# An attention and FP4 feed-forward layer, tile by tile: turning the quantised codes with a transposing DMA instead of TensorE, and moving three small pieces of work between engines

## The reference

```
q = elu(x Wq + bq) + 1;  k = elu(x Wk + bk) + 1, each head scaled to length 1;  v = x Wv + bv
attn = (q k^T) v per head of 16;  y = x + attn Wo + bo
x1 = layernorm(x + (layernorm(y, 1e-6) * gamma + beta))
fq(a): per block of 16 along the last axis: scale = max|a| / 6; each a/scale rounded to 0, .5, 1, 1.5, 2, 3, 4, 6 with its sign; times scale
h = silu(fq(x1) fq(w_gate)^T) * (fq(x1) fq(w_up)^T)        # 704 wide
out = layernorm(x1 + fq(h) fq(w_down)^T)
```

## Time and profile before

| | |
|---|---|
| median of 3 runs | 700.19 us (700.13 to 703.07) |
| the profiled execution | 700.59 us, of which 698.9 us from the first to the last instruction |
| busy PE, DVE, ACT, Pool | 683.4, 584.1, 489.3, 608.8 us |
| DMA traffic | 56.36 MB |
| granted TensorE clock | 0.998 of full |

### The profile page before, as it was taken

How to read it: one execution, slowest core, us unless ns; L and a number is a source line. 1 busy time by engine, 2 the same in 40 slices (tenths; PEclk the granted TensorE clock), 3 DMA queues, 4 the chain that set the end, 5 groups by cost and what they waited for, 6 DMA issues and landing times.

```text
span 698.9 us, 14240 instructions
## 1 busy us (share of the span) xinstructions
PE 683.4 (98%) x4370; PEld 602.8 (86%) x4370; DVE 584.1 (84%) x1441; ACT 489.3 (70%) x954; POOL 608.8 (87%) x947
## 2 busy tenths in 40 slices
PE   8999999999989999999999999999999999999995
PEld 6888888888868799999999999999999999999995
DVE  6678678876778899889989998998998998998774
ACT  4677777766777676777677677677767767767664
POOL 3988898988888998899989989899899988989766
PEclk9999999999999999999999999999999999999999
DMA  8544443344301111122211122122111211100001
GB/s 267 189 136 136 136 140 117 131 157 155 107 32 34 58 47 46 45 78 75 76 66 57 36 86 80 57 76 76 46 61 62 77 45 47 61 17 16 21 28 45
DMA packets 23135, 56.36 MB, mean 81 GB/s; under 512 B 2642, under 2 KB 5908, under 8 KB 23060
## 3 DMA queue, kind: packets, MB, share of 16 engines
q1 hardware_dynamic: 22640, 55.32, 23.4%
q10 hardware_dynamic: 420, 0.13, 0.1%
HBM read 30.22 MB, written 25.17 MB: 79 GB/s over the span
## 4 chain that ended last, share of the span: by engine, by line
PE 91%; DVE 2%; POOL 2%; issue 2%; ACT 1%; DMA 1%; SPq 0%; POOLq 0%; DVEq 0%
PE banks L407 23%; PE banks L408 22%; PE banks L409 22%; PE banks L553 8%; PE banks L524 7%; PE banks L445 2%; PE banks L418 2%; PE banks L567 1%; PE banks L566 1%; PE banks L431 1%; PE banks L476 1%; DMA arena<-in_L_attn_x_dram 1%; PE banks L484 1%; POOL arena L1164 1%; DVE actT_lo L958 0%
## 5 line engine op out<-in xcount | busy, mean ns | idle before, releaser
L407 PE MATMUL banks<-wgu_hi,actT_lo 128*128 128x512 f32 (+1 forms) x384 | 149.8, 390 | 1.6 <-DVE actT_lo L958 1.4
L408 PE MATMUL banks<-wgu_lo,actT_hi 128*128 128x512 f32 (+1 forms) x384 | 144.0, 375 | 0.0
L409 PE MATMUL banks<-wgu_hi,actT_hi 128*128 128x512 f32 (+1 forms) x384 | 143.3, 373 | 0.0
L725 ACT ACTIVATE arena<-banks 128x512 f32<-128x512 f32 x64 | 38.4, 600 | 111.8 <-PE banks L409 111.6
L1164 POOL TENSOR_TENSOR arena<-arena 128x960 f32<-128x960 f16 (+2 forms) x68 | 115.3, 1695 | 0.0
L1140 POOL TENSOR_TENSOR arena<-arena 128x704 f32<-128x704 f32 x64 | 91.8, 1434 | 20.5 <-DVE arena L945 18.6
L407 PE MATMUL banks<-wd_hi,actT_lo 128*128 128x256 f32 x320 | 100.1, 313 | 0.0
L958 DVE TENSOR_TENSOR actT_lo<-banks,actT_hi 128x512 fp32r<-128x512 f32 (+1 forms) x132 | 85.5, 674 | 16.9 <-ACT actT_hi L711 16.2
L409 PE MATMUL banks<-wd_hi,actT_hi 128*128 128x256 f32 x320 | 90.2, 282 | 0.0
L408 PE MATMUL banks<-wd_lo,actT_hi 128*128 128x256 f32 x320 | 90.2, 282 | 0.0
L407 PEld LDWEIGHTS banks<-wgu_hi,actT_lo 128*128 128x128 f32 x384 | 72.5, 189 | 11.2 <-DVE actT_lo L958 2.3
(11 more groups left out here) (126 smaller groups left out, 1917.3 us busy)
## 6 DMA issues: line engine op xcount, KB each, us to landing
xs<-x_plus_scratch SPq DMA_DIRECT2D x32, 512.0 KB, 3.3
x_plus_scratch<-xs SPq DMA_DIRECT2D x24, 512.0 KB, 2.9
arena<-in_L_attn_x_dram SPq DMA_DIRECT2D x32, 256.0 KB, 3.5
out_dram<-arena SPq DMA_DIRECT2D x32, 256.0 KB, 2.1
x_plus_scratch<-arena SPq DMA_DIRECT2D x4, 512.0 KB, 2.9
x_plus_scratch<-resid SPq DMA_DIRECT2D x4, 512.0 KB, 2.6
resid<-in_L_attn_x_dram SPq DMA_DIRECT2D x4, 256.0 KB, 3.9
resid<-in_L_ffn_w_down_dram SPq DMA_DIRECT2D x1, 704.0 KB, 8.0
```

What stands on the lines that cost most here:

```text
L407: nc.tensor.matmul(dst, sl, mh, start=(k == 0), stop=False, skip_group_check=shared)
L408: nc.tensor.matmul(dst, sh, ml, start=False, stop=False, skip_group_check=shared)
L409: last = nc.tensor.matmul(dst, sh, mh, start=False, stop=(ended and k == n - 1), skip_group_check=shared)
```

## The change

From tile 14 on (`BY_DMA = 14`, `by_dma(n)`), the codes are turned before they are dequantised. `cut` writes all 1024 columns (ACT makes the doubled last 64 too). SP issues one transposing DMA of the 128 x 1024 codes, 16 bits each, from `vqc` into `codes`. The scales must then lie in the turned form as well: PE turns `s14` (one transpose, `scales_turn`), ACT copies it to SBUF (`scales_copy`), SP stores it to DRAM in three DMAs, waits for them, and loads it back with each scale repeated over 16 partitions as a full 128 x 1024 operand (`spread_scales`). Pool multiplies `codes` by it into `va`'s place (`dequantise_turned`), ACT makes the high part from SBUF at the head of its next step (`high_turned`), and DVE the low part in one subtraction (`low_turned`). PE's eight transposes of the tile go, and `attend` moves ahead of `gate_up` part 2.

For all tiles: `residual` moves from DVE to ACT and becomes a copy of x1 into the down product's bank ahead of the product, which then accumulates on top of it; statistics and the last layernorm read that bank. `down_begin` is two matmuls once. Of Pool's four root operations the sum with epsilon goes to DVE (`root_sums`, behind low) and the negated means to ACT (`root_means`, behind the second silu).

```diff
+        BY_DMA = 14
+        codes = wo_sb[:, :, :].rearrange("p k d -> p (k d)").bitcast(U16).rearrange("p (c n) -> p c n", c=VC)
+        s_each = [resid[:, 4 * i:4 * i + 4, :].rearrange("p t d -> p (t d)").rearrange("p (c n) -> p c n", c=VC)
+                  for i in range(2)]
@@ SP, at the end of step(t)
+                if by_dma(t + 2):
+                    turn_codes(t + 2)
+                if by_dma(t + 3):
+                    spread_scales(t + 3)
+            def turn_codes(n):
+                sp.wait_ge(round_s, n + 1)
+                sp.wait_ge(deq_s, n)
+                sp.dma_start_transpose(codes, vqc[n % 2].bitcast(U16)).then_inc(codes_in, 16)
+            def spread_scales(n):
+                i = n - BY_DMA
+                sp.wait_ge(sT_s, i + 1)
+                after(sp, s_each_in[n % 2], 16 * (i // 2))
+                whole = (VC - 1) * GC
+                sp.dma_start(s_turned[n % 2, :, 0:VC - 1, :].rearrange("g c t -> c g t"),
+                             sT[0:whole, :]).then_inc(sT_out, 16)
+                half = GC // 2
+                for k in range(2):
+                    sp.dma_start(s_turned[n % 2, k * half:(k + 1) * half, VC - 1, :],
+                                 sT[whole:whole + half, :]).then_inc(sT_out, 16)
+                sp.wait_ge(sT_out, 3 * 16 * (i + 1))
+                if i < 2:
+                    sp.wait_ge(r3_s, 4 * i + 4)
+                sp.wait_ge(deq_s, n - 1)
+                sp.dma_start(s_each[n % 2].rearrange("p c n -> p (c n)"),
+                             s_turned[n % 2].rearrange("g c t -> g (c t)").unsqueeze(1).broadcast_to(
+                                 [GC, BLK, VC * P])).then_inc(s_each_in[n % 2], 16)
@@ PE
+            def scales_turn(n):
+                pe.wait_ge(scale_s, n + 1)
+                after(pe, sT_s, n - BY_DMA)
+                nc.tensor.transpose(ps[0:VB, T_BANK, 0:P], s14[:, n % 2, :], ident[:, :]).then_inc(sT_ps, 1)
             def down(t):
-                after(pe, r3_s, t - 1)
+                pe.wait_ge(r3_s, t + 1)
@@ PE step(t), behind gate_up parts 0 and 1
+                if by_dma(t + 3):
+                    scales_turn(t + 3)
-                if joint(t + 1):
+                if joint(t + 1) and not by_dma(t + 1):
                     turn(t + 1)
+                if by_dma(t + 1) and there(t + 9):
+                    attend(t + 9)
                 if there(t):
                     gate_up(t, 2)
@@ ACT
+            def scales_copy(n):
+                act.wait_ge(sT_ps, n - BY_DMA + 1)
+                after(act, sT_out, 3 * 16 * (n - BY_DMA))
+                nc.scalar.activation(sT[0:VB, :], ps[0:VB, T_BANK, 0:P], ACT.Copy).then_inc(sT_s, 1)
+            def high_turned(n):
+                act.wait_ge(deq_s, n + 1)
+                if there(n - 2):
+                    act.wait_ge(gu_ps, 3 * n - 3)
+                act.wait_ge(dn_ps, n - 1 - LAG)
+                a, v = chunks(n)[0], v_turned(n)
+                nc.scalar.activation(vT_hi[:, n % 2, a:VC - 1, :], v[:, a:VC - 1, :], ACT.Copy).then_inc(vT_hi_s, 1)
+                nc.scalar.activation(vT_hi[:, n % 2, VC - 1, :], v[:, VC - 1, :], ACT.Copy,
+                                     scale=upper[:, :]).then_inc(vT_hi_s, 1)
+            def residual(u):
+                act.wait_ge(x1_s, u + 1)
+                after(act, ob_s, u - 1)
+                nc.scalar.activation(ps[:, DN_BANK[u % 2], 0:D], resid[:, u, :], ACT.Copy).then_inc(r3_s, 1)
+            def root_means(t):
+                act.wait_ge(agg_s, aggregated(t - 1))
+                after(act, root_s, rooted(t - 1))
+                nc.scalar.activation(nm[:, :], mv[:, t % 2, :, 0], ACT.Copy, scale=-1.0).then_inc(nm_s, 1)
@@ DVE
+            def low_turned(n):
+                a, v = chunks(n)[0], v_turned(n)
+                dve.wait_ge(vT_hi_s, 2 * n + 2)
+                nc.vector.tensor_tensor(vT_lo[:, n % 2, a:VC, :], v[:, a:VC, :], f32(vT_hi[:, n % 2, a:VC, :]),
+                                        ALU.subtract).then_inc(vT_lo_s, 1)
+            def root_sums(t):
+                dve.wait_ge(agg_s, aggregated(t - 1))
+                after(dve, pow_s, rooted(t - 1))
+                nc.vector.tensor_tensor(ve[:, :], mv[:, t % 2, :, 1], eps_v[:, :], ALU.add).then_inc(ve_s, 1)
@@ DVE step(t), behind the aggregates
+                if by_dma(t + 1):
+                    low_turned(t + 1)
+                elif joint(t + 1):
                     low(t + 1)
+                if t + 1 >= FIRST + 2:
+                    root_sums(t + 1)
@@ Pool
+            def dequantise_turned(n):
+                a = chunks(n)[0]
+                pool.wait_ge(codes_in, 16 * (n - BY_DMA + 1))
+                pool.wait_ge(s_each_in[n % 2], 16 * ((n - BY_DMA) // 2 + 1))
+                pool.wait_ge(vT_lo_s, n - 1)
+                nc.gpsimd.tensor_tensor(v_turned(n)[:, a:VC, :], codes[:, a:VC, :].bitcast(F16), s_each[n % 2][:, a:VC, :],
+                                        ALU.mult).then_inc(deq_s, 1)
```

More of the change, by code:

```diff
@@ L54, in build @@
     x_plus = nc.dram_tensor("x_plus_scratch", (NP, P, 4 * D), F32, kind="Internal").ap()
+    GC = P // BLK
+    s_turned = nc.dram_tensor("scales_scratch", (2, GC, VC, P), F32, kind="Internal").ap()
     with ExitStack() as ctx:
@@ L260, in joint, with by_dma @@
             return there(n) or there(n - LAG)
+        def by_dma(n):
+            return joint(n) and n >= BY_DMA
         def columns(n):
@@ L303, in build @@
         DEFER = NP - 4
-        X_AGAIN = {14 + 8 * i: DEFER + i for i in range(NP - DEFER)}
+        X_AGAIN = {21 + 6 * i: DEFER + i for i in range(NP - DEFER)}
         def x_biases_free(eng, p):
@@ L402, in _, with split_product @@
         def _(pe):
-            def split_product(dst, stat, mov, n, ended=True, shared=False):
+            def split_product(dst, stat, mov, n, ended=True, shared=False, begun=False):
                 for k in range(n):
                     (sh, sl), (mh, ml) = stat(k), mov(k)
-                    nc.tensor.matmul(dst, sl, mh, start=(k == 0), stop=False, skip_group_check=shared)
+                    nc.tensor.matmul(dst, sl, mh, start=(k == 0 and not begun), stop=False, skip_group_check=shared)
                     nc.tensor.matmul(dst, sh, ml, start=False, stop=False, skip_group_check=shared)
@@ L511, in first, with down_begin @@
                     weights_turn(WG_STEP[p])
+            def down_begin():
+                pe.wait_ge(mo_sb, B)
+                for bank in DN_BANK:
+                    last = nc.tensor.matmul(ps[:, bank, 0:D], wd_hi[:, 0, 0:P], wd_hi[:, 0, :], start=True, stop=True)
+                last.then_inc(dn_free, 1)
             def attend(u):
@@ L551, in turn @@
                 after(pe, vT_lo_s, n)
+                after(pe, sT_s, n + 3 - BY_DMA)
                 for c in range(c0, c1):
@@ L574, in step @@
                     gate_up(t, 1)
-                if joint(t + 1):
+                if by_dma(t + 3):
+                    scales_turn(t + 3)
+                if joint(t + 1) and not by_dma(t + 1):
                     turn(t + 1)
+                if by_dma(t + 1) and there(t + 9):
+                    attend(t + 9)
                 if there(t):
                     gate_up(t, 2)
-                if there(t + 9):
+                if not by_dma(t + 1) and there(t + 9):
                     attend(t + 9)
+                if t == LAG - 1:
+                    down_begin()
                 if there(t - LAG):
@@ L696, in to_f16 @@
                 after(act, round_s, n - 1)
+                if by_dma(n):
+                    nc.scalar.activation(vqb[n % 2][:, RN, 0:RW].bitcast(F16), halves(vy[:, n % 2, VW - RW:VW]), ACT.Copy,
+                                         scale=F16_ONE)
                 nc.scalar.activation(vqb[n % 2][:, a // RW:b // RW, 0:RW].bitcast(F16), lines(halves(vy[:, n % 2, a:b])),
@@ L757, in step @@
                     ln3_apply(t - 6, t)
-                if joint(t + 1):
+                if there(t - LAG):
+                    residual(t - LAG)
+                if by_dma(t + 3):
+                    scales_copy(t + 3)
+                if joint(t + 1) and not by_dma(t + 1):
                     high(t + 1)
@@ L761, in step @@
                     silu(t, 1)
+                if FIRST + 2 <= t + 1 <= LAST + 1:
+                    root_means(t + 1)
                 if joint(t + 3) and not pair(t + 33):
@@ L970, in gated @@
                                             ALU.mult).then_inc(h_s, 1)
-            def residual(u):
-                dve.wait_ge(dn_ps, u + 1)
-                after(dve, ob_s, u - 1)
-                nc.vector.tensor_tensor(r3[:, u % 2, :], ps[:, DN_BANK[u % 2], 0:D], resid[:, u, :], ALU.add).then_inc(r3_s, 1)
             def ln1_sum(u):
@@ L990, in step @@
                 have = aggregated(t - 1)
-                if n3:
-                    residual(t - 5)
                 if joint(t + 2):
@@ L999, in step @@
                 if n3:
```

(9 more changed lines are left out.)

40 lines of the change are left out of this document (23 added, 17 removed).

## The result

The changed kernel takes 835.14 us (median of 4 runs, 834.25 to 836.03) against 701.31 us of the kernel before beside it: ratio 1.191, 95% interval 1.187 to 1.194. It is slower, as forecast, by 134 us and not by 60: the time lies above the whole range of 698 to 788. Where single executions of a kernel fell far above its others (two of the four of x1, 1136 and 1375 us, and one of the eight of x18, 734 us), they are left out of its time here, and no trace shows why they were slow.

What follows compares the result with a forecast made beforehand. PE bounded the old step at 7.57 us; the DVE-Pool lock chain would make it 8.9. 44 such steps cost 58 us, the last six 3; 700.59 + 61 = 762, median 761, range 698 to 788.

Steps and rivals of the forecast that it cites:

- the port: SBUF port shared by DVE and Pool; forecast to make them exclude each other for whole operations, deciding the step.
- the lock: Exclusion between Pool and DVE operations with two SBUF inputs, held for the whole instruction; about 1.0 us on Pool's dequantise.
- Part 1: PE's step: eight transposes go, one of the scales returns; 7.57 falls to 6.80 us.
- Part 2: ACT's step: four new small operations raise 5.42 to about 6.8 us, bounds 6.2 to 7.1, hidden by waits for PE.
- Part 3: Pool's own work: dequantise_turned at 2.3 us replaces 2.30 us of removed operations; 6.9, with short waits 7.0 us.
- Part 4: DVE's own work: low_turned 1.16 us, cut 0.04 more, residual gone; 6.94 falls to about 6.7 us.
- Part 5: DVE and Pool holding the port in turn: low_turned delays dequantise, root_sums waits behind it; step 8.9 us.
- A: Likeliest case: root_sums waits for Pool's whole dequantise, lasting 2 us or more; step 8.9, 761 us; chance 0.38.
- B: Same lock, milder phase: root_sums waits behind a short operation, about 0.5 to 0.8; step 7.95, 719 us; chance 0.27.
- Part 6: DMAs: codes land in 3.4 us, within 3.8 allowed; scales' way takes some 8 us, needed 12 later; no cost.
- Rival D: Slow transposing DMA, 8 to 9 us, in a ring of two steps; step 9.6, 789 us; chance 0.14.

Runs made afterwards that it cites:

- x1: Changed kernel with no tile turned by DMA, the other moved parts kept; 715.6 us.
- x18: x16 with joint_scales no longer waiting for Pool's multiplication and the scales copied earlier; 704.5 us.
- x22: x21 with the 512 KB scales' load left out from the third turned tile on, stores and SP's wait for them kept; 747.5 us.
- x2: Changed kernel with scales spread for the first two turned tiles only, then reused; codes still turned by DMA; 743.6 us.
- x16: x13 with the turning DMA put back; 719.8 us.
- x13: x6 with the root sum on ACT, the cut in 13 and 3 rows, and attend back at its old place; 678.9 us.
- x4: Changed kernel with low_turned taking one operand from an idle PSUM bank and the root sum one input; 835.9 us.
- x17: x1 with both root operations on ACT and root_means behind k_exps while the keys' projections run; 704.9 us.
- x6: Changed kernel with codes taken unturned, scales of the first two turned tiles reused, low part from idle PSUM, one-input root sum; 718.1 us.
- x21: Changed kernel, but from the third turned tile the scales' load lands where nobody reads and Pool reuses earlier scales; 839.2 us.
- x8: x1 with the root sum as two operations of one SBUF input each instead of one with two; 716.0 us.

## Why the prediction was wrong

The loss, taken apart run by run: the scales' load 88 to 92 us (x22), their stores 4 (x2), the port and the operations that came late 24 (x16), the turning DMA 41 (x13), and against these the 22 us that the engines alone gain. 701.3 + 92 + 24 + 41 - 22 = 836, with the stores within the 92; since each run is the one before it with more left out, the sum has to come out. The order matters: taken first, the port is worth nothing (x4). That the change came out slower, as forecast, is partly luck: taking away the lock, on which the forecast rests, changes nothing in the change as it is (x4), and most of the loss comes from a step that the forecast cleared.

- **Part 1, PE: right.** 6.80 us forecast; Pool's L1274 in x13 stands at 453.47 and 460.27, 6.80 apart, with PE busy for all of it. The 44 full steps there average 6.84.
- **Part 2, ACT: the sum right, the order missed.** ACT's work in x13 is 186.51/200 of 6.80, 6.3 us, in its bounds of 6.2 to 7.1. But I said that it costs nothing while the waits for PE cover it, and looked only at the tile loop; ahead of it root_means stood in front of k_exps and cost 5.8 us (x17).
- **Part 3, Pool: a little high.** dequantise_turned takes 2.15, forecast 2.3, and 2.00 in x13. Pool's work there is 190.85/200 of 6.80, 6.5 us, where I had 6.9; so PE sets that step and not Pool.
- **Part 4, DVE:** low_turned was forecast at 1.16. In the change it takes 1.37 in the median; the 1.19 of x16 is with one operand in PSUM. The cut was costed at 0.04 more and became 0.28 shorter, but it is now an operation that Pool can hold, up to 1.6 us (x6).
- **Part 5, the port: right as a mechanism, wrong as the bound.** A's wait shows in x1 (1.5 us) and in B's form in x2 (8.09 us a step against 7.95). In the change itself root sums read 0.69 in the median, B's sign and not A's 2 us, and Pool's wait for the codes, 125.3 us, is the sign that I had named for Part 6 being wrong.
- **Part 6, the DMAs: this step failed.** I wrote "I take 3.4" for the landing of the codes, from transfers of a kernel whose DMA engines were busy for a fifth, and cleared the scales' way by its length alone: "some 8 us, needed 12 us later". That Pool would not wait for them was even right (x21). What I did not price is that this load, 512 KB in every step, lies beside the turning: alone the turning lands in 3.1, in the change in 5.8 in the median and 6.2 on average, up to 10.0. Each transfer was costed alone, though the change takes the DMA share from 0.2 to 0.7.
- **Rival D** had the mechanism, with 0.14, and the wrong ring. I spread it over two steps, (6.8 + 0.65 + 2.3 + 0.3 + T)/2. But joint_scales waits for Pool's multiplication and stands ahead of the cut, so it closes in one: 2.15 + 1.39 + 0.07 + T. With T = 5.8 mine gives 7.9; this one, in which T averages 6.21 over the full steps, closes at their 9.82. The 44 full steps cost 44 x (9.82 - 7.57) = 99 us, where A's sum had 58; the last steps cost 23, where it had 3; and 11 are lost ahead of them, where it had nothing. Of these 11 the moved parts alone lose 10 by the same step (x1).
- The Trainium skill's rate for transposes (DMA: Bandwidth & Descriptors, "Latency and other measured facts"), by which I estimated 1.0 us for these 256 KB, is short of the 3.1 measured alone, and so is the estimate of 2.2 from it and a second page. In x22 the packets take 1.4 of the 3.1 in the median; the rest passes before the first and behind the last. The measurement decides.

## What to carry to other kernels

Price a new transfer twice: by its own time, and by what it does to the one beside it that somebody waits for. When an operation moves, walk the in-order queue in every phase in which it runs, not only in the loop that is costed. And before a wait is blamed, send the data elsewhere with the traffic kept (x21): leaving the transfer out altogether (x2) looks the same for both theories. That a wait stands last on the chain is not enough: the load there had ended 3.1 us before Pool started.

## What I had not expected of the hardware

- A DVE tensor_scalar of two or three elements with a single SBUF input is held behind a Pool instruction: 1463 ns in the median for two (x8), 1452 for three (x6). Of one element, directly ahead of it in x8, it is not: 140 to 154 ns in all 78. Nor are the reciprocal (530 at most, x6) and the reductions (889 at most for 704 columns, x1).
- The 16-bit cut over 15 rows of 64 takes 0.64 us and over 16 rows, though it is larger, 0.36. But this one can be held by Pool, up to 1.61 us (x6), and Pool's L1245 beside it reads 0.31 in the median where it read 0.20 before. In 13 and 3 rows the cut takes 0.57 and 0.20 and is not held (0.65 and 0.25 at most, x13).
- After waits of PE its clock falls for a while. In the change PE stands for 2.0 us up to 503.32 and for 0.7 more up to 504.34; from 505.0 to 508.4 the granted clock is 0.5, the lower of its two levels (1.2 of 2.4 GHz), and a 384-column matmul takes 0.53 us instead of 0.34. From 400 to 500 us 0.86 is granted on average. PE is not in the ring of the codes; whether the lower clock costs anything no run here tests.
